# Swin block: the masked key blocks of the transposed scores stored token by token instead of window by window

## The reference

```python
xn = ln(x, norm1_g, norm1_b)
xw = windows(roll(xn, (-3, -3)))                       # (1024, 49, 48)
q, k, v = split(xw @ qkv_w + qkv_b)                    # 6 heads of 8
attn = softmax(q * 8**-0.5 @ k.T + rpb + MASK)
out = unroll(attn @ v) @ proj_w + proj_b
x1 = x + out
y = x1 + gelu(ln(x1) @ fc1_w + fc1_b) @ fc2_w + fc2_b
```

## Time and profile before

| what | value |
|---|---|
| time, median of 2 runs | 1102.08 us (1100.97 to 1103.18) |
| time of the profiled execution | 1103.58 us |
| its span, first to last instruction | 1101.8 us |
| granted clock of the matrix engine, mean | 0.977 |
| PE busy | 948.9 us (86%) |
| PEld busy | 753.7 us (68%) |
| DVE busy | 915.0 us (83%) |
| ACT busy | 775.7 us (70%) |
| POOL busy | 810.7 us (74%) |

### The profile page before, as it was taken

One profiled execution on the slowest core, in us unless ns is written; L12 is line 12 of the kernel. 1 busy time (PEld: TensorE's weight loads), 2 busy tenths in 40 slices (PEclk: granted clock), 3 DMA queues, 4 the chain that ended last, 5 costly groups with the idle time before them and its releaser, 6 DMA issues. The chain is left out here.

```text
span 1101.8 us, 45568 instructions
## 1 busy us (share of the span) xinstructions
PE 948.9 (86%) x16004; PEld 753.7 (68%) x16004; DVE 915.0 (83%) x2136; ACT 775.7 (70%) x1730; POOL 810.7 (74%) x971
## 2 busy tenths in 40 slices
PE   0489999999999999999999999999992877777777
PEld 0267878887888778788878887887871445554444
DVE  5678888888888888888888888888855999999997
ACT  0468887887788788878878887887852555555554
POOL 6257777777777777777777777777764888888884
PEclk9989999999999999999999999999995799999999
DMA  1022222222222222222222222222210333334333
GB/s 53 28 70 69 69 75 70 62 73 72 66 64 75 72 61 69 74 68 61 73 72 66 65 75 72 61 76 75 55 45 15 80 89 91 93 90 94 91 89 87
DMA packets 139237, 77.32 MB, mean 70 GB/s; under 512 B 105923, under 2 KB 138980, under 8 KB 139190
## 3 DMA queue, kind: packets, MB, share of 16 engines
q1 hardware_dynamic: 86966, 63.83, 21.9%
q10 hardware_dynamic: 52224, 12.85, 6.1%
HBM read 10.48 MB, written 9.63 MB: 18 GB/s over the span
## 5 line engine op out<-in xcount | busy, mean ns | idle before, releaser
L389 POOL TENSOR_TENSOR pl<-p 113x294 f16<-113x294 f32 x512 | 348.3, 692 | 47.1 <-ACT p L456 35.6
L232 POOL TENSOR_TENSOR rstd<-var,mhalf 112x7 f32<-112x7 f32 x128 | 193.1, 1509 | 94.6 <-ACT var L227 81.9
L456 ACT ACTIVATE p<-banks 113x294 f32<-113x294 f32 x512 | 214.8, 419 | 51.3 <-PE banks L631 41.0
L615 PE MATMUL banks<-Qh,KAg 128*128 128x147 f16 x2048 | 218.4, 228 | 0.0
L777 DVE TENSOR_REDUCE rowmax<-banks 113x12 f32<-113x588 f32 x256 | 192.6, 752 | 10.2 <-PE banks L598 8.7
L615 PEld LDWEIGHTS banks<-Qh,KAg 128*128 128x128 f16 x2048 | 167.1, 97 | 31.1
L631 PE MATMUL banks<-Vb,p 113*128 113x36 f16 x3072 | 175.5, 180 | 0.5 <-POOL pl L389 0.5
L584 PE MATMUL banks<-bs_h,idt 113*128 113x294 f16 x512 | 146.1, 293 | 30.8 <-DVE QAg L771 25.1
L631 PE MATMUL banks<-Vb,pl 113*128 113x36 f16 x1536 | 162.8, 180 | 0.0
L631 PEld LDWEIGHTS banks<-Vb,p 113*128 113x128 bf16 x3072 | 156.5, 97 | 0.7 <-POOL pl L389 0.7
L584 PE MATMUL banks<-bt_h,idt 113*128 113x294 f16 x512 | 148.5, 290 | 3.8 <-DMA Qh<-mT 3.8
(11 more groups left out here) (126 smaller groups left out, 2587.8 us busy)
## 6 DMA issues: line engine op xcount, KB each, us to landing
Qh<-QAB SPq DMA_DIRECT2D x192, 98.0 KB, 2.2
Vb<-Vn SPq DMA_DIRECT2D x256, 54.0 KB, 2.1
xres<-in_x SPq DMA_DIRECT2D x64, 147.0 KB, 2.2
KAh<-KA SPq DMA_DIRECT2D x192, 49.0 KB, 1.9
out_y<-ybuf SPq DMA_DIRECT2D x64, 147.0 KB, 2.0
Qh<-mT SPq DMA_DIRECT2D x128, 4.6 KB, 2.2
hT<-xtok ACTq DMA_TRANSPOSE x32, 2.8
hT<-htok ACTq DMA_TRANSPOSE x32, 2.8
```

The lines of the kernel that those rows point to most:

```text
L232: nc.gpsimd.tensor_tensor(rstd[:, :], var[:, :], mhalf[:, :], ALU.pow).then_inc(s_pow, 1)
L389: nc.gpsimd.tensor_tensor(pl[p % 4][:, :, :, 0:N].rearrange("p a w n -> p (a w) n"), p32[p % 4][:, :, :, 0:N].rearrange("p a w n -> p (a w ...
L456: nc.scalar.activation(p32[p % 4][:, :, :, 0:N].rearrange("p a w n -> p w a n"), src, ACT.Exp, scale=1.0 / SB).then_inc(s_exp, 1)
L615: i = nc.tensor.matmul(bank[:, w * COLS:(w + 1) * COLS], KAg[upar][:, 2 * p + w, :, :].rearrange("p g n -> p (g n)"), Qh[upar][:, level, : ...
```

## The change

The buffer `KAg` gets another order of its elements within a row: group, token, window instead of window, group, token. Its size, its rows and its values stay the same. ACT's two instructions read `KA` as before and still go window by window, token by token; their writes now land 16 elements of 2 bytes, 32 bytes, apart, and start one element further for the next window. PE's load of one window's block takes 128 elements that stand 32 bytes apart instead of 128 neighbouring ones. No instruction is added or taken away, and no wait, no order and no DMA is changed.

```diff
-        KAg = [sba(f"KAg{i}", [FULL, UW, G, GP], f16) for i in range(2)]
+        KAg = [sba(f"KAg{i}", [FULL, G, GP, UW], f16) for i in range(2)]
...
-                    nc.scalar.activation(KAg[par][:, :, 0, 0:N], KA[par][:, :, :], ACT.Copy,
+                    nc.scalar.activation(KAg[par][:, 0, 0:N, :].rearrange("p n w -> p w n"), KA[par][:, :, :], ACT.Copy,
                                          scale=grow[:, 0:1]).then_inc(s_kg[0], 1)
...
-                    nc.scalar.activation(KAg[par][:, :, 1, 0:N], KA[par][:, :, :], ACT.Copy,
+                    nc.scalar.activation(KAg[par][:, 1, 0:N, :].rearrange("p n w -> p w n"), KA[par][:, :, :], ACT.Copy,
                                          scale=grow[:, 1:2]).then_inc(s_kg[1], 1)
...
                             i = nc.tensor.matmul(bank[:, w * COLS:(w + 1) * COLS],
-                                                 KAg[upar][:, 2 * p + w, :, :].rearrange("p g n -> p (g n)"),
+                                                 KAg[upar][:, :, :, 2 * p + w].rearrange("p g n -> p (g n)"),
                                                  Qh[upar][:, level, :, 2 * p + w, :], start=False, stop=True, skip_group_check=True)
```

## The result

The changed kernel takes 1520.65 us (median of 2 runs, 1520.36 to 1520.94) against 1102.08: a ratio of 1.380, 95% interval 1.374 to 1.386. The forecast of 1178 had the sign, the place and the mechanism, but the loss is 418.6 us where it said 76, and the time lies far above the range.

The account below looks back on a forecast made before the run. Bound: the slackless chain from PE's key piece through ACT and DVE back to PE, 12.14 us a step. ACT's writes add 62 x 1.22 = 75.6 us, loads 0, on the profiled 1103.58: 1179, said as 1178; range 1099 to 1195.

Parts of the forecast that it names:

- The chain without slack: PE's key piece, ACT's run with both `KAg` instructions, DVE, `x_transposes`: added ACT time delays each step fully, 1.22 us.
- The rival by which ACT's idle time takes the extra time up: ACT's idle time in the attention step absorbs the slower writes; time stays at 1102; chance 0.28, shared with nothing slowing.
- The loads hide behind their products: Line 615's weight loads at 32 bytes stay covered by products 65 ns apart; claimed cost 0.
- The second: Rival: line 615's loads slow but ACT's write does not; 1102 + 29 = 1131 us; chance 0.09.
- the fourth rival: Line 615's loads slow to several times their 96 ns; 1200 to 1350 us; chance 0.08.
- the third: Rival: both ACT's write and line 615's loads slow, the loads adding 6 us; 1184 us; chance 0.12.
- The price of ACT's write: Lines 480 and 489: 0.78 ns more an element, 610 ns for each instruction, 1.22 us a step.
- the upper bound: ACT's two `KAg` writes: at most one more 0.85 ns pace an element, 664 ns each, 82 us in all.
- The clock: Risk that PE, waiting 1.2 us a step, is granted less than 1.00; not contained in the sum.

Follow-up runs that it names:

- the run with the filled wait: Changed kernel plus 60 identity products that serve nothing, on PE ahead of `x_transposes` in each step; 1441.76 us, ratio 1.309 to the kernel before.
- 4 bytes between the writes: Changed kernel with `KAg` in blocks of two windows instead of 16, so writes and weight loads step 4 bytes; 1122.38 us.
- the run with the loads alone: Kernel before, writes still packed, but line 615 loads its weights from a cleared buffer at the 32-byte step; 1110.15 us, ratio 1.008.
- the kernel with packed loads: Changed kernel, but ACT's 32-byte-step writes go to a second buffer nobody reads and PE loads packed zero weights from `KAg`; 1502.05 us.
- the run with 4-byte elements: Kernel before, but ACT writes 4-byte elements 32 bytes apart into a buffer nobody reads; PE's packed weights are zero; 1181.47 us.

## Why the prediction was wrong

*The chain without slack* was right in the main. Between the first and the last instruction of group 0, 63 steps, it is 758.3 us in the kernel before and 1088.8 (1139.8 - 51.0) in the run with the filled wait: 330.5 us or 5.25 us a step, where the two instructions grew by (3734 - 953) + (3716 - 962) = 5535 ns. With 4 bytes between the writes it is 776.9 (826.4 - 49.5), 0.30 us a step for a growth of (1218 - 953) + (1243 - 962) = 546 ns. So some 0.25 to 0.3 us a step do not come back, which the prediction had not seen. `ln_low` is 0.07 of it (0.51 us instead of 0.58); the rest was not followed up. The rival by which ACT's idle time takes the extra time up is refuted, at this place and at the end of the step.

*The loads hide behind their products:* right, by the run with the loads alone. There the load shown grew from 96 to 144 ns and its product did not wait. The second and the fourth rival are out; of the third no more can be true than fits into what stays open below.

*The price of ACT's write* is the step that failed: "0.78 x 784 = 610 ns for each instruction" was (3731 - 953) = 2778 and (3654 - 962) = 2692 ns by the means of lines 480 and 489, 3.5 ns an element. The row from which it came, DVE's copy at line 865, had a far step but 4-byte elements. For such elements ACT shows (1717 - 953) / 784 = 0.97 ns, not far from the 0.78, although the engine is another and DVE's pace of 0.93 ns came from line 840, which reads every third number: the row was no row for lone 2-byte writes. And the upper bound, one more turn of the pace, was not a bound; no row excluded more. The rule of the Trainium skill's page "SBUF — State Buffer" (Specifications) that a 16-byte line wants at least two hits has the right line, as 16 and 32 bytes cost the same here and the price at 16, 8 and 4 bytes goes by the number of lines. It does not have the size of the piece: two hits 8 bytes apart were still 2.1 us, two neighbouring ones 0.94.

*The clock* was named as a risk and left out of the sum, that is, put at nothing. The wait of 3.45 us a step made PE's clock fall: filled with work, with the 1.4 us wait ahead of it left as it was, the clock stayed at 1.00 and 78.9 us came back.

The sum with the measured terms: in 62 steps the chain grew by 62 x 5.27 = 327 us and the part behind it by 62 x 1.37 = 85, together 412 of the 418.6. The runs say the same between the first and the last instruction of group 0: 1219.2 - 49.0 = 1170.2 us in the changed kernel, 411.9 more than before, of which the run with the filled wait leaves 330.5 and takes away 81.4.

Open: why the kernel with packed loads was 18.6 us faster than the changed one, although the loads alone cost nothing in the attention phase. Its two instructions are shorter by (3734 - 3640) + (3648 - 3606) = 136 ns a step, 8.4 us. The other half lies behind `x_transposes`, where PE runs at its lower level: in the two traces the way from there to the next `k_high(1)` is 0.15 us shorter in the mean of 61 steps. Why was not tried, and its weights were zero.

## What to carry to other kernels

When an edit gives an instruction a form that the trace doesn't hold, a row that shares the step but not the element size bounds nothing. Where ACT writes apart, try to write at least two neighbouring 16-bit numbers at a time, and let the weight loads, which had cover, take the far step. A wait that is not listed can still be the tight one: where a consumer starts the same 0.05 us behind its producer in every step, the chain has no slack for more, and pulling a piece out of it may pay if the same chain feeds another wait, as here that for `QAg`: 3.2%. A wait of 3.45 us on a full matrix engine was paid twice here, once as the wait and once in the clock behind it; a wait of some 1.2 us a step in the run with 4-byte elements left the granted clock at 1.00.

## What the runs showed of the hardware that was not expected

- A lone 2-byte write of ACT costs 4.3 to 4.5 ns for each 16-byte line that it goes to, above some 0.34 us for the instruction (3.73 us for 784 at 32 bytes, 3.83 at 16, 2.10 at 8, 1.22 at 4, 0.95 packed); a 4-byte write about 1.8 ns at 32 bytes (1.72 us for 784); pairs of 2 bytes at 64 bytes nothing that can be seen (0.94 us for 768).
- ACT's reads of 2-byte elements 98 bytes apart cost 1.36 ns more each (2.02 us for 784).
- Weight loads of 128 columns are shown with 96 ns packed, 97 at 4 bytes from column to column, 113 at 8, 145 at 16 and 144 at 32 (the run with the loads alone); products that start 65 ns apart hid even the last entirely.
- After 3.45 us of waiting PE's granted clock was 0.50 for the next 3.5 us of dense work; 60 products that serve nothing, put into that wait, kept it at 1.00 and took 78.9 us off the time.
